# Clearing four accumulators: when the clears are issued, and in what order the first sums use them

## The reference

```
xn  = layernorm(x)
gnn = segment_sum(edge_weight[:, None] * (xn @ weight_l)[dst], src, 12500) + bias_l + xn @ weight_r + bias_r
mix = (attention_over_features(xn) * gate(xn)) @ Wproj + bproj
x1  = x + gnn + mix
out = x1 + top_2_of_8_experts(layernorm(x1))
```

## Time and profile before

| what | value |
| --- | --- |
| median of 3 runs | 4441.68 us (4427.51 to 4441.93) |
| the profiled execution, its own time | 4410.35 us |
| its span, first to last instruction | 4408.4 us |
| POOL busy | 3117.6 us (71% of the span) |
| PE busy | 3387.8 us (77%) |
| DVE busy | 2647.6 us (60%) |
| ACT busy | 1660.1 us (38%) |
| setup phase | to 63.6 us |
| first addition of a message | at 152.5 us |
| last addition of a message | at 3250.1 us |

### The profile page before, as it was taken

One profiled execution on the slowest core, in us unless ns is written; L12 is line 12 of the kernel. 1 busy time (PEld: TensorE's weight loads), 2 busy tenths in 40 slices (PEclk: granted clock), 3 DMA queues, 4 the chain that ended last, 5 costly groups with the idle time before them and its releaser, 6 DMA issues. The chain is left out here.

```text
span 4408.4 us, 85937 instructions
## 1 busy us (share of the span) xinstructions
PE 3387.8 (77%) x16649; PEld 2799.6 (64%) x16650; DVE 2647.6 (60%) x11867; ACT 1660.1 (38%) x3046; POOL 3117.6 (71%) x2089
## 2 busy tenths in 40 slices
PE   1467666666676767788888878888768869999999
PEld 1355555555555555666666666666557758888888
DVE  3577777665565555666666666666547764444444
ACT  1233333244444443444444444444311113333333
POOL 0588888888888888888888888888855554444444
PEclk7788788787888888888888888888879989999999
DMA  8889888877777777777777777777779866666665
GB/s 364 260 162 174 170 159 170 170 123 116 116 109 117 116 107 114 108 108 104 106 108 108 101 108 108 103 106 109 92 178 274 253 204 142 138 143 142 141 141 116
DMA packets 573617, 637.99 MB, mean 145 GB/s; under 512 B 59217, under 2 KB 534251, under 8 KB 571857
## 3 DMA queue, kind: packets, MB, share of 16 engines
q0 software_dynamic: 279264, 270.04, 49.3%
q1 hardware_dynamic: 246752, 260.61, 20.0%
q10 hardware_dynamic: 47504, 106.29, 6.3%
HBM read 248.34 MB, written 390.31 MB: 145 GB/s over the span
## 5 line engine op out<-in xcount | busy, mean ns | idle before, releaser
L849 POOL DMA_INDIRECT agg<-msg,sidx x1664 | 2584.0, 1553 | 661.9 <-issue 408.5
L1153 PE MATMUL bank<-rows,Cmat 128*128 x3328 | 1026.6, 450 | 166.4 <-ACT msg L1346 141.4
L1346 ACT COPY msg<-bank 128x512 f32<-128x512 f32 x832 | 487.1, 585 | 1477.3 <-DMA agg<-msg,sidx 1211.2
L1153 PEld LDWEIGHTS bank<-rows,Cmat 128*128 128x128 f32 x3328 | 699.8, 225 | 347.8 <-issue 254.6
L904 DVE SCALAR_TENSOR_TENSOR sidx<-seen_sum,trash,srcf 128x4 int32<-128x4 f32 x416 | 92.7, 223 | 1018.1 <-DMA agg<-msg,sidx 1011.7
L2169 POOL DMA_INDIRECT out_dram<-x_y,x_node x210 | 334.4, 1592 | 456.9 <-DVE x_y L2137 376.4
L887 DVE TENSOR_SCALAR Emat<-bank,srcf,wtf 128x128 f32<-128x128 f32 x1664 | 565.5, 401 | 0.0
L1137 PEld LDWEIGHTS bank<-Emat,pick 128*128 128x128 f32 x3328 | 514.1, 225 | 40.6 <-issue 16.2
L1128 PE MATMUL bank<-packed,both 128*128 (+1 forms) x416 | 185.9, 447 | 446.0 <-DVE seen L891 427.1
L1137 PE MATMUL bank<-Emat,pick 128*128 128x128 f32 x3328 | 525.2, 310 | 1.7 <-DVE seen L891 1.7
L891 DVE SCALAR_TENSOR_TENSOR seen<-bank,srcf,prior 128x128 f32<-128x128 f32 x1664 | 480.8, 345 | 0.0
(11 more groups left out here) (260 smaller groups left out, 4311.6 us busy)
## 6 DMA issues: line engine op xcount, KB each, us to landing
x_w<-in_L_ffn_W_dram SPq DMA_DIRECT2D x105, 512.0 KB, 4.4
agg<-expert_rows ACTq DMA_DIRECT2D x12, 4224.0 KB, 58.7
r_agg<-agg SPq DMA_DIRECT2D x196, 256.0 KB
x_rows<-expert_rows_table SPq DMA_DIRECT2D x105, 261.0 KB, 4.6
window_raw<-in_x_dram SPq DMA_DIRECT2D x208, 128.0 KB, 2.5
agg<-msg,sidx POOLq DMA_INDIRECT x1664, 3.8
xn_rows<-n_xn ACTq DMA_DIRECT2D x49, 256.0 KB
xn_turned<-n_xnT ACTq DMA_DIRECT2D x49, 256.0 KB
```

Source lines behind the costliest of these rows:

```text
L849: pool.indirect_dma_start(scratch["agg"][r][:, :], bass.IndirectOffsetOnAxis(ap=sidx[:, j:j + 1], axis=0), msg[:, j % (2 * BATCH), :], Non ...
L1153: mm = nc.tensor.matmul(M[p][:, (q % 2) * D:(q % 2 + 1) * D], Cmat[:, b % 2, q, :], rows[:, bass.ds(slot, 1), :], start=True, stop=True)
L1346: nc.scalar.copy(msg[:, at:at + 2, :].rearrange("p q c -> p (q c)"), M[p][:, :]).then_inc(s_msg, 1)
```

## The change

The clears no longer wait for the weights: ACT issues the first seven when `zeros` is ready. Each accumulator gets its own semaphore. In group 0 the sixteen chunks use the accumulators in the order 0, 1, 2, 0, 1, 2, 0, 3 and then 0 to 3 twice, and each accumulator's first addition waits for its own three clears alone; all later counts are shifted by what accumulator 0 has more and accumulator 3 has less. The weights are loaded in another order, the small ones first; there is still one semaphore for all. In group 0, DVE's statistics of x move from places 2 and 3 to 10 and 11 and its normalising of x from 10 and 11 to 14 and 15; ACT's deviations go from 1 to 11, and turning and keys, on PE and ACT, all go to place 15.

```
-        weights = [(wq), (wk), (wv), (wproj), (wg1), (wg2), (wr), (bg1), (bias_l), (bias_r), (bproj)]
+        weights = [(bg1), (bias_l), (bias_r), (bproj), (wg1), (wq), (wg2), (wk), (wv), (wproj), (wr)]
...
-        clears = [(acc, n) for acc in scratch["agg"] for n in range(CLEARS)]
+        clears = [(r, n) for r in range(NACC) for n in range(CLEARS)]
...
             act.wait_ge(s_clear, 5)
-            act.wait_ge(s_w, WEIGHTS)
-            act.nop(nofuse=True)
-            for acc, n in clears[:READY]:
-                act.dma_start(clear_rows(acc, n), zeros).then_inc(s_zeroed, 16)
+            for r, n in clears[:READY]:
+                act.dma_start(clear_rows(scratch["agg"][r], n), zeros).then_inc(s_zeroed[r], 16)
...
+FIRST_GROUP = (0, 1, 2, 0, 1, 2, 0, 3) + 2 * tuple(range(NACC))
+SHIFT = tuple(FIRST_GROUP.count(r) - len(FIRST_GROUP) // NACC for r in range(NACC))
...
-                    if not (first(g) and b == 0):
-                        pool.wait_ge(s_add[r], 16 * (NB * g + b))
+                    if first(g):
+                        r = FIRST_GROUP[j]
+                        if r not in FIRST_GROUP[:j]:
+                            pool.wait_ge(s_zeroed[r], 16 * CLEARS)
+                        else:
+                            pool.wait_ge(s_add[r], 16 * FIRST_GROUP[:j].count(r))
+                    else:
+                        pool.wait_ge(s_add[r], 16 * (NB * g + b + SHIFT[r]))
...
             gather(0, 1)
-            pool.wait_ge(s_zeroed, 16 * NACC * CLEARS)
-            pool.nop(nofuse=True)
             group(0)
...
-                steps = [(2 + u, lambda u=u: statistics(n, u)) for u in pairs_of(n)]
-                steps += [(10 + u, lambda u=u: normalise(n, u)) for u in pairs_of(n)]
+                steps = [((10 if first(n) else 2) + u, lambda u=u: statistics(n, u)) for u in pairs_of(n)]
+                steps += [((14 if first(n) else 10) + u, lambda u=u: normalise(n, u)) for u in pairs_of(n)]
...
-                    steps += [(5 + 4 * u, lambda u=u: turn(n, u)), (8 + 4 * u, lambda u=u: keys(n, u))]
+                    steps += [(15 if first(n) else 5 + 4 * u, lambda u=u: turn(n, u)),
+                              (15 if first(n) else 8 + 4 * u, lambda u=u: keys(n, u))]
...
-                    for r in (2 * p, 2 * p + 1):
-                        act.wait_ge(s_add[r], 16 * (nb - 1))
+                    if first(g):
+                        for r in set(FIRST_GROUP[:BATCH * (b - 1)]):
+                            act.wait_ge(s_add[r], 16 * FIRST_GROUP[:BATCH * (b - 1)].count(r))
+                    else:
+                        for r in (2 * p, 2 * p + 1):
+                            act.wait_ge(s_add[r], 16 * (nb - 1 + SHIFT[r]))
...
-                steps = [(1, lambda u=u: deviations(n, u)) for u in pairs_of(n)] + [(8, lambda: blank_out(n))]
+                steps = [(11 if first(n) else 1, lambda u=u: deviations(n, u)) for u in pairs_of(n)] + [(8, lambda: blank_out(n))]
```

More of the change, by code:

```diff
@@ L120, in build @@
                    wg2=sb("wg2", [GH, D]), bg2h=sb("bg2h", [P, HALF]), hbias=sb("hbias", [P, GH]), bsum=sb("bsum", [1, D]))
-        s_zeroed = sem("accumulators_cleared")
+        s_zeroed = [sem(f"accumulator_cleared{r}") for r in range(NACC)]
         setup_phase(nc, t, scratch, psum, ident, prior, trash, iota8, ones, zeros,
@@ L204, in setup_phase @@
                  for n, a in enumerate((t["L0_mix_ln_g"], t["L0_mix_ln_b"], t["L0_mix_bg2"]))]
-        weights = [(mix["wq"][:], halves(t["L0_mix_Wqkv"][:, 0:D])), (mix["wk"][:], halves(t["L0_mix_Wqkv"][:, D:2 * D])),
-                   (mix["wv"][:], halves(t["L0_mix_Wqkv"][:, 2 * D:3 * D])), (mix["wproj"][:], halves(t["L0_mix_Wproj"])),
[L207 to L211, removed]
+        weights = [(mix["bg1"][:], row(t["L0_mix_bg1"])),
+                   (mix["brows"][:, 0, :], row(t["L0_gnn_bias_l"])), (mix["brows"][:, 1, :], row(t["L0_gnn_bias_r"])),
+                   (mix["brows"][:, 2, :], row(t["L0_mix_bproj"])),
+                   (mix["wg1"][:], halves(t["L0_mix_Wg1"])), (mix["wq"][:], halves(t["L0_mix_Wqkv"][:, 0:D])),
+                   (mix["wg2"][:], t["L0_mix_Wg2"]), (mix["wk"][:], halves(t["L0_mix_Wqkv"][:, D:2 * D])),
+                   (mix["wv"][:], halves(t["L0_mix_Wqkv"][:, 2 * D:3 * D])), (mix["wproj"][:], halves(t["L0_mix_Wproj"])),
+                   (mix["wr"][:], halves(t["L0_gnn_weight_r"]))]
         WEIGHTS = 16 * len(weights)
-        clears = [(acc, n) for acc in scratch["agg"] for n in range(CLEARS)]
+        clears = [(r, n) for r in range(NACC) for n in range(CLEARS)]
         READY = 7
@@ L279, in _ @@
             nc.scalar.copy(edges["packed"][:], wide[:])
-            for acc, n in clears[READY:]:
-                act.dma_start(clear_rows(acc, n), zeros).then_inc(s_zeroed, 16)
+            for r, n in clears[READY:]:
+                act.dma_start(clear_rows(scratch["agg"][r], n), zeros).then_inc(s_zeroed[r], 16)
             act.wait_ge(s_pprep, 2)
@@ L455, in first @@
     return isinstance(i, int) and i == 0
+FIRST_GROUP = (0, 1, 2, 0, 1, 2, 0, 3) + 2 * tuple(range(NACC))
+SHIFT = tuple(FIRST_GROUP.count(r) - len(FIRST_GROUP) // NACC for r in range(NACC))
+assert len(FIRST_GROUP) == CHUNK_GROUP and SHIFT == (1, 0, 0, -1)
 def edge_phase(nc, t, scratch, psum, ident, prior, trash, ones, gscale, edges, mix, ffn, zeros, out, s_zeroed):
@@ L748, in _ @@
                 normal_turn(n)
-            sp.wait_ge(s_zeroed, 16 * NACC * CLEARS)
+            for r in range(NACC):
+                sp.wait_ge(s_zeroed[r], 16 * CLEARS)
             sp.nop(nofuse=True)
@@ L864, in _ @@
             for r in range(NACC):
-                pool.wait_ge(s_add[r], 16 * CHUNKS // NACC)
+                pool.wait_ge(s_add[r], 16 * (CHUNKS // NACC + SHIFT[r]))
         @block.vector
@@ L901, in add_rows @@
                     for r in range(NACC):
-                        dve.wait_ge(s_add[r], 16 * (nb - 3))
+                        dve.wait_ge(s_add[r], 16 * (nb - 3 + (SHIFT[r] if b else max(SHIFT[r], 0))))
                 cols = slice(BATCH * b, BATCH * (b + 1))
@@ L1444, in normal_steps @@
             def normal_steps(n):
-                steps = [(1, lambda u=u: deviations(n, u)) for u in pairs_of(n)] + [(8, lambda: blank_out(n))]
+                steps = [(11 if first(n) else 1, lambda u=u: deviations(n, u)) for u in pairs_of(n)] + [(8, lambda: blank_out(n))]
                 for u in pairs_of(n):
-                    steps += [(6 + 4 * u, lambda u=u: turned_out(n, u)), (10 + 4 * u, lambda u=u: keys_out(n, u))]
+                    steps += [(15 if first(n) else 6 + 4 * u, lambda u=u: turned_out(n, u)),
+                              (15 if first(n) else 10 + 4 * u, lambda u=u: keys_out(n, u))]
                 return steps
```

## The result

The changed kernel takes 4602.55 us (median of 5 runs, 4598.33 to 4605.99), against 4441.68 us (median of 5 runs, 4427.51 to 4445.77) for the kernel before. The ratio is 1.036, with an interval of 1.0346 to 1.0373. The prediction was 4439 us, 3 us less than before, with a range of 4414 to 4453. It missed by 164 us and in the sign: the kernel became 161 us slower.

The account below looks back on a forecast made before the run. POOL's additions at a fixed 1.85 us each were taken to bound the edge phase; chunk 12, 3.1 us earlier, was to pass to the end, 4441.68 - 3 = 4439 us, range 4414 to 4453.

Parts of the forecast that it names:

- The shifted counts cost nothing.: Waits on the accumulators: the counts shifted for the new order of accumulators were to add no time.
- to the end one for one: Edge phase: POOL adds at a fixed 1.85 us each, so any gain before that pace reaches the end in full.
- The steps up to the first addition: Setup phase and group 0: weights at 81 us, first window load at 105.5, first addition at 145 against 152.49.
- the rivals: Setup: weights hidden 0.22, 4423 us; partly hidden 0.15, 4435; engine 0 gap 0.15, 4448; engine 0 not behind 0.05, 4413.
- the weights were held back: Setup phase: beside the clears the weights land at 81 us, so DVE passes its wait 41 us later than 39.74.
- fifteen engines ran dry: Between early and late clears: all DMA engines but engine 0 have no work for 8 to 11 us.
- Chunk 8 and chunk 12: Marks in group 0: added at 162 us against 169.41 and at 173.8 us against 176.93.
- W: Group 0: arrival of the next group's window 0, which only the end of the clears frees, at 152 us.
- Slower by over 0.5%: Whole kernel: chance 0.03 of a loss over 0.5%, for which the weights would have to land near 108 us.
- late weights: Setup phase: weights landing after about 87 us decide for a loss; with a gap, at 93 us, 4448 us, chance 0.15.
- One row for one: DMA queues beside clears: each small row of q1 waits for one clear row of q10, 1.21 to 1.29 us each.
- engine 0's tail: Setup loads: rests of 31 rows lie on one engine until 23.3 us, so its clears start only 3.4 us earlier.

Follow-up runs that it names:

- e1_exact: The changed kernel with the exact count in DVE's wait at batch 0, group 1 written out ahead of the loop; 4443.60 us, ratio 0.9995.
- e2_late3: The kernel before with only the surplus count of one addition on accumulator 3 in DVE's wait at batch 0; 4591.83 us, ratio 1.033.
- e3_exact_hold: The changed kernel with the exact count, and its clears waiting for the weights again; 4434.66 us, ratio 0.9974.
- e5_hold_split: e3_exact_hold with each rest of 31 rows of the edge list loaded as 16 and 15 rows; 4395.11 us, ratio 0.9962.
- e6_early_split: e1_exact with each rest of 31 rows loaded as 16 and 15 rows, clears not waiting for the weights; 4391.42 us, ratio 0.9952.

## Why the prediction was wrong

**The step that failed** is the sentence that closes the parts of the change: "The shifted counts cost nothing." The cost is 160 us, of which e1_exact removes all and e2_late3 alone shows 146. The prediction took the shifts of all counts as equivalent and read none of them as an inequality. It also stopped at chunk 16 and passed what came before "to the end one for one", by a pace that it took from before; but an added wait that stands in a loop has to be checked in a group of each stage. What the runs showed in place of "nothing": a wait for chunk 7 where chunk 3 is enough, which makes a group take 33.9 us instead of 29.7 while x is normalised, and 30.6 instead of 29.6 beside the mix.

**What the earlier trace rows really said.** That POOL idled on nothing but issue ahead of 1336 additions shows that it was fed in time. It doesn't say by how much. The cover of DVE's wait, which is what the change used up, is found elsewhere. The view that the earlier trace rows is cut from also lists who waited for these additions, and there stands, before the change:

```profile
  DVE sidx L904: 1011.7, 389
```

Ahead of 389 of DVE's 416 steps at this line its idle time ended with the landing of an addition, 1011.7 us in all (3.06 us of it in the row above). So this wait held DVE in nearly every batch, and any lengthening of it delays DVE at once. The loop, from landing to DVE, PE, ACT and back to POOL, had little to spare although no engine of it was busy all the time.

**The steps up to the first addition** were right, most of them within 1 us, by the table above. So was the choice among the rivals: the weights were held back (DVE passed at 82.72 us), fifteen engines ran dry (share 0.06), and the clears' wait was replaced by one for messages. Two slips did no harm: twelve clears of 4.33 MB are 51.9 MB and 122 us at 427 GB/s, not 50.7 MB and 119 us, but the sum goes by the 124.5 us measured; and 13.5 + 71.7 is 85 us, not 87, for the end of the seven clears on fifteen engines.

**Chunk 8 and chunk 12** came 3.4 and 3.0 us later than forecast. 1.4 us of both is the later window (153.36). The rest is the way from W to the message, counted too short: chunk 8 came at W + 12.1 where I had 10, chunk 12 at W + 23.4 where I had 21.8. The forecast of 3 us less is one for the change without the surplus count, and that is e1_exact: 6.7 us less to 2.2 us more. It holds both my 3 us and no change, so these runs can't tell the two apart.

**Chances.** "Slower by over 0.5%" had 0.03, all of it put on late weights. No case for a fault in a count was on the list.

## What to carry to other kernels

When the order of shared buffers changes, write down for each wait which item it asks for, before and after, and hold it against the item that it needs: a count that is one too high gives no wrong result as long as it is still reached, and it is paid in each turn of the loop in which the wait has no cover. A producer that never starves says nothing on how late its suppliers may be; read the slack on the engine whose wait is moved, in each stage of the loop, and in the list of those who wait for the bottleneck. And to put something in front earlier gains only if what it pushes back isn't needed sooner: here the clears went out 13 us earlier and pushed DVE's step behind the weights back by 43.

## What the runs showed of the hardware that was not expected

**Additions beside clears.** In e3_exact_hold chunks 3, 4 and 5 are added 11 us apart, and the idle time ended on a landing (rows of chunks 0 to 5):

```profile
107.56 1.70 POOL L862 DMA_INDIRECT agg<-msg,sidx  x1 [101.84 <-ACT msg L1363]
109.56 1.55 POOL L862 DMA_INDIRECT agg<-msg,sidx  x1 [0.30 <-issue]
121.87 1.54 POOL L862 DMA_INDIRECT agg<-msg,sidx  x1 [10.75 <-issue]
125.56 1.55 POOL L862 DMA_INDIRECT agg<-msg,sidx  x1 [2.15 <-DMA agg<-msg,sidx]
136.76 1.54 POOL L862 DMA_INDIRECT agg<-msg,sidx  x1 [9.65 <-DMA agg<-msg,sidx]
147.68 1.54 POOL L862 DMA_INDIRECT agg<-msg,sidx  x1 [9.38 <-DMA agg<-msg,sidx]
```

By the order 0, 1, 2, 0, 1, 2 these three wait for chunks 0, 1 and 2. So POOL could go on some 18, 27 and 26 us after the start of the addition that it waited for; in the steady state DVE could go on after 4.0 to 5.8 us (the rows of DVE above). So 45 us of head start (107.56 against 152.49) became 9 us at chunk 12 (168.02 against 176.93). What exactly holds an addition up beside the clears isn't shown.

**Rows on one engine.** With 31 rows in one piece, the kernel before had one engine of 16 at work from 18.0 to 23.3 us, and its clears, held for the weights, were issued at 25.82 us. With 16 and 15 rows, and the clears held in the same way, e5_hold_split issues them at 18.06 us:

```profile
18.06 7.09 ACTq L269 DMA_DIRECT2D agg<-expert_rows  x7
```

The Trainium skill (DMA: Bandwidth & Descriptors, "Why a DMA increments its semaphore by 16 and not by 1") has a transfer on as many engines, up to 16, as divide its rows, so that 31 rows are on one and 16 and 15 on sixteen and fifteen. The trace agrees: e3_exact_hold, which differs by the split alone, issues its clears at 25.51 us, 7.5 us later.

**One row for one, and a case without it.** Packets of the queues from 13 to 35 us (packets, MB, share of 16 engines), in the changed kernel and in e6_early_split:

```profile
q10 hardware_dynamic: 353, 8.61, 91.0%
q1 hardware_dynamic: 507, 0.49, 7.3%
```

```profile
q10 hardware_dynamic: 265, 8.41, 88.7%
q1 hardware_dynamic: 1111, 1.05, 16.5%
```

In the second, q1 has 4.2 packets for each of q10, and the weights were in early. But that is no rate at which an engine takes turns: 996 of the 1111 came from 13 to 16 us, some 62 for each engine, when q10 had one packet in all, although its clears had been issued from 12.12 us on. So the weights went ahead of the clears, not between their rows. Where both queues had work for long, in the changed kernel from 35 to 60 us, they had 351 and 351. The Trainium skill (DMA: Bandwidth & Descriptors, "Queues, rings and completion order") has an engine drain a whole packet, typically 9 to 17 descriptors, before it turns to the other queue. The 351 and 351 speak against it, and 62 for each engine with hardly a row of a clear between them are far more. What let the weights go first in e6_early_split wasn't tried and stays open; so does whether the split works there by engine 0's tail or by this.
